# Cross-attention by pairs of heads on two row halves, with its projections interleaved in a new order

## What is computed

```python
def xattn(x, context):                       # x (4, 256, 128) normalised, context (4, 512, 256)
    q = split_heads(x @ Wq)                  # 16 heads of 64
    k, v = split(context @ Wkv)              # each (4, 16, 512, 64)
    k, v = concat(null_k, k), concat(null_v, v)        # one more key and value for every head
    attn = softmax(q * 64 ** -0.5 @ k.T)
    out = merge_heads(attn @ v) @ Wout
    return layernorm(out) * ln_scale + ln_bias
x = x + xattn(layernorm(x), ctx)
x = x + ffn(layernorm(x))                    # self-attention, router, 8 experts, top 2
```

## Time and profile before

| | us |
|---|---|
| median of 3 runs (715.19 to 719.41) | 719.25 |
| the profiled execution, its span | 711.4 |
| PE recorded busy | 602.2 (85%) |
| DVE | 587.9 (83%) |
| ACT | 454.6 (64%) |
| POOL | 227.9 (32%) |

### The profile page before, as it was taken

One profiled execution on the slowest core, in us unless ns is written; L12 is line 12 of the kernel. 1 busy time (PEld: TensorE's weight loads), 2 busy tenths in 40 slices (PEclk: granted clock), 3 DMA queues, 4 the chain that ended last, 5 costly groups with the idle time before them and its releaser, 6 DMA issues. The chain is left out here.

```text
span 711.4 us, 13311 instructions
## 1 busy us (share of the span) xinstructions
PE 602.2 (85%) x3580; PEld 492.3 (69%) x3580; DVE 587.9 (83%) x1282; ACT 454.6 (64%) x1094; POOL 227.9 (32%) x435
## 2 busy tenths in 40 slices
PE   2979889988999999899999336899997689797996
PEld 2757778767887778778787325666666577575885
DVE  4768899878898788998889747899983599979995
ACT  3657777766777677767777125888883356344563
POOL 1553334323333333333335354722132321414000
PEclk9989999999999999999999868999998699998999
DMA  8020000000000000000000002000000220200000
GB/s 255 17 54 2 2 29 3 1 1 0 0 30 0 1 0 0 0 0 1 1 1 1 1 4 82 1 1 0 0 0 1 78 77 2 77 1 0 0 0 29
DMA packets 15342, 13.48 MB, mean 19 GB/s; under 512 B 1984, under 2 KB 14656, under 8 KB 15296
## 3 DMA queue, kind: packets, MB, share of 16 engines
q1 hardware_dynamic: 15072, 12.94, 6.2%
q10 hardware_dynamic: 224, 0.03, 0.0%
HBM read 12.44 MB, written 0.52 MB: 18 GB/s over the span
## 5 line engine op out<-in xcount | busy, mean ns | idle before, releaser
L516 ACT ACTIVATE p_raw<-bank,bias 128x512 f32<-128x512 f32 x128 | 87.7, 688 | 43.1 <-DVE bias L587 39.4
L582 DVE TENSOR_REDUCE neg_max<-bank 128x1 f32<-128x512 f32 x128 | 86.9, 679 | 5.9 <-issue 4.0
L657 POOL TENSOR_SCALAR p_norm<-p_raw,rinv 128x512 f32<-128x512 f32 x128 | 87.0, 692 | 0.1
L606 DVE TENSOR_TENSOR pT_lo<-bank,pT_hi 128x512 fp32r<-128x512 f32 x128 | 82.4, 685 | 3.9 <-issue 2.3
L534 ACT ACTIVATE pT_hi<-bank 128x512 fp32r<-128x512 f32 x128 | 69.7, 599 | 24.9 <-PE bank L439 23.4
L1472 ACT ACTIVATE act_hi<-act_f 128x512 fp32r<-128x512 f32 x56 | 35.4, 632 | 58.9 <-DVE act_f L1515 58.8
L439 PE MATMUL bank<-ident,p_norm 128*128 128x128 f32 x512 | 66.8, 273 | 0.4 <-DVE pT_lo L606 0.4
L439 PEld LDWEIGHTS bank<-ident,p_norm 128*128 128x128 f32 x512 | 59.8, 141 | 9.3 <-issue 1.2
L451 PE MATMUL bank<-pT_hi,vals 128*128 128x256 f32 x256 | 64.9, 286 | 1.5 <-DVE o_lo L598 1.5
L451 PE MATMUL bank<-pT_lo,vals 128*128 128x256 f32 x256 | 64.0, 283 | 0.0
L426 PE MATMUL bank<-keys,q_hi 128*128 128x512 f32 x128 | 54.7, 427 | 3.0 <-ACT p_raw L516 2.8
(11 more groups left out here) (272 smaller groups left out, 1731.3 us busy)
## 6 DMA issues: line engine op xcount, KB each, us to landing
ctx_raw<-in_ctx SPq DMA_DIRECT2D x4, 512.0 KB, 4.7
wkv_raw<-in_L_xattn_Wkv SPq DMA_DIRECT2D x2, 1024.0 KB, 11.1
gu_raw<-in_L_ffn_w_gate SPq DMA_DIRECT2D x4, 448.0 KB, 3.6
gu_raw<-in_L_ffn_w_up SPq DMA_DIRECT2D x4, 448.0 KB, 4.3
dn_raw<-in_L_ffn_w_down SPq DMA_DIRECT2D x4, 448.0 KB, 5.1
wout_raw<-in_L_xattn_Wout SPq DMA_DIRECT2D x2, 512.0 KB, 14.8
x<-in_x SPq DMA_DIRECT2D x1, 512.0 KB, 6.8
wq_raw<-in_L_xattn_Wq SPq DMA_DIRECT2D x1, 512.0 KB, 10.2
```

Of the source, the lines that this page charges most:

```text
L516: act.activation(p_raw[:, h % 2, t, :], s_bank[t][:, :], ACT.Exp, bias=bias[:, h % H, t:t + 1], scale=X_SCALE, accum_out=row_sum[:, h % H, ...
L582: dve.tensor_reduce(neg_max[:, h % H, t:t + 1], s_bank[t][:, :], AX_X, ALU.max, negate=True).then_inc(max_s, 1)
L606: dve.tensor_tensor(pT_lo[:, h % 2, 2 * half:2 * half + 2, :], t_bank[half][:, :].rearrange("p (j n) -> p j n", j=2), f(pT_hi[:, h % 2, 2 ...
L657: pool.tensor_scalar(p_norm[:, h % 2, t, :], p_raw[:, h % 2, t, :], rinv[:, h % H, t:t + 1], 1.0, ALU.mult, ALU.mult).then_inc(p_norm_s, 1)
```

## The change

The cross-attention works on pairs of heads g (32 of them) in steps, with two heads of a pair on partitions 0 to 63 and 64 to 127.

- Query weights are stored once; one projection gives both heads' queries. Keys are kept as `keys_hi` and `keys_lo`, 8 tiles of two heads each. Scores are three matmuls of 64 rows for each head and token tile, alternating between the two heads, into two of four score banks.
- The two halves of the weighted values are copied by ACT (`o_copy`), added by DVE (`o_halves`) and split by GpSimd (`o_split`). The output projection runs for four pairs at once, in every fourth step, with `y_copy` by ACT for the first half of a batch and `y_add` by DVE for the second. The output weights are stored once.
- Every step with a successor projects one key unit and one value unit, four pairs ahead; queries, keys, values and context share `unit_bank`. For values ACT makes the high part and DVE the low part.
- The bias and the null terms are computed for two heads in one instruction. Probabilities are normalised in place.
- The loops over batches are written out on all engines. In the load stage the first key units are four instead of three, the splits of Wq and Wout have half the size, Wout is loaded once, and the null value's product has 8 matmuls of 128 rows instead of 16 of 64.

```diff
-            k.wq_hi, k.wq_lo = (sw(f"wq_{s}", [P, H, 2, DH]) for s in ("hi", "lo"))
+            k.wq_hi, k.wq_lo = (sw(f"wq_{s}", [P, H, DH]) for s in ("hi", "lo"))
-            k.wout_hi, k.wout_lo = (sw(f"wout_{s}", [P, H, D]) for s in ("hi", "lo"))
+            k.wout_hi, k.wout_lo = (sw(f"wout_{s}", [P, HP, D]) for s in ("hi", "lo"))
-            k.keys = sw("keys", [P, H, M])
+            k.keys_hi, k.keys_lo = (sw(f"keys_{s}", [P, HP, M]) for s in ("hi", "lo"))
...
-        s_bank, t_bank, y_bank, proj_bank = banks[0:2], banks[2:4], banks[6], banks[7]
-        q_whole, q_bank, o_bank = banks[4], banks[4][:, 0:N], banks[5][:, 0:N]
+        s_bank, t_bank, unit_bank, out_bank = banks[0:4], banks[4:6], banks[6], banks[7]
+        o_part, y_part = out_bank[:, 0:N], out_bank[:, N:2 * N]
+        AHEAD = HP // 2
+        QUART = 4
+        STEPS = range(-2, NP + 3)
...
+            def project_q(g):
...
+                b = g // HP
+                if unit_at(g - 2) is not None:
+                    pe.wait_ge(v_lo_s, g - 1)
+                elif g >= 1:
+                    pe.wait_ge(q_lo_s, g)
+                for i, (w, x) in enumerate(((k.wq_hi, k.xnT_hi), (k.wq_hi, k.xnT_lo), (k.wq_lo, k.xnT_hi))):
+                    last = pe.matmul(unit_bank[:, 0:N], w[:, columns(g), :].rearrange("p h d -> p (h d)"), x[:, b * N:(b + 1) * N],
+                                     start=i == 0, stop=i == 2)
+                last.then_inc(q_ps, 1)
...
+            def keys_unit(g):
...
+                pe.wait_ge(q_lo_s, g + 2)
+                if n // HP >= 1:
+                    pe.wait_ge(c_lo_s, n // HP * CT)
+                project(pe, k, "k", n % HP, 0, unit_bank).then_inc(k_ps, 1)
...
+            def values_unit(g):
...
+                pe.wait_ge(k_lo_s, g + 1)
+                project(pe, k, "v", n % HP // KT, n % KT, unit_bank).then_inc(v_ps, 1)
...
+            def scores(g, t):
...
+                G = 2 * g + t
+                if t == 0:
+                    pe.wait_ge(q_lo_s, g + 1)
+                    if g >= AHEAD:
+                        pe.wait_ge(k_lo_s, g - AHEAD + 1)
+                if G >= 2:
+                    pe.wait_ge(p_exp, 2 * G - 2)
+                for m, (q, keys) in enumerate(((q_hi, k.keys_hi), (q_lo, k.keys_hi), (q_hi, k.keys_lo))):
+                    for i in range(2):
+                        last = pe.matmul(score_bank(G, i)[:, :], q[rows(i), g % 2, t * P:(t + 1) * P], keys[rows(i), g % HP, :],
+                                         start=m == 0, stop=m == 2)
+                        if m == 2:
+                            last.then_inc(s_ps, 1)
...
+            def weighted_values(g, i):
...
+                pe.wait_ge(t_lo_s, 4 * g + 2 * i + 2)
...
+                if 2 * g + i >= 1:
+                    pe.wait_ge(o_raw_s, 2 * g + i)
...
+                for kt in range(KT):
+                    for n, x in enumerate((pT_hi, pT_lo)):
+                        last = pe.matmul(o_part, k.vals[:, kt, 2 * (g % HP) + i, :], x[:, i, kt, :],
+                                         start=kt == 0 and n == 0, stop=kt == KT - 1 and n == 1)
+                last.then_inc(o_ps, 1)
...
+            def project_out(s):
+
...
+                for j in range(QUART):
+                    g = QUART * m + j
...
+                    for n, (w, x) in enumerate(((k.wout_hi, o_hi), (k.wout_hi, o_lo), (k.wout_lo, o_hi))):
+                        last = pe.matmul(y_part, w[:, g % HP, :], x[:, g % O_KEPT, :], start=j == 0 and n == 0,
+                                         stop=m % 2 == 0 and j == QUART - 1 and n == 2)
...
+                last.then_inc(y_ps, 1)
...
+            for s in STEPS:
+                transpose_probs(s - 1, 1, 1)
+                if not after_context(s):
+                    keys_unit(s)
+                scores(s + 1, 1)
+                transpose_probs(s, 0, 0)
+                transpose_probs(s, 0, 1)
+                project_out(s)
+                if after_context(s):
+                    keys_unit(s)
+                    weighted_values(s - 1, 1)
+                    values_unit(s)
+                else:
+                    values_unit(s)
+                    weighted_values(s - 1, 1)
+                transpose_probs(s, 1, 0)
+                project_q(s + 2)
+                null_probs(s)
+                context_unit(s, 0)
+                weighted_values(s, 0)
+                scores(s + 2, 0)
+                context_unit(s, 1)
...
+            def values_head(g):
...
+                i, t = n % HP // KT, n % KT
+                act.wait_ge(v_ps, g + 1)
+                if n >= HP:
+                    act.wait_ge(o_ps, 2 * (n // KT * KT - KT))
+                act.activation(values_of(k, i, t, 0), by_head(unit_bank[:, :]), ACT.Copy).then_inc(v_hi_s, 1)
...
+            def o_copy(g, i):
...
+                act.wait_ge(o_ps, 2 * g + i + 1)
+                if g >= 2:
+                    act.wait_ge(o_sum_s, 2 * (g - 2) + i + 1)
+                act.activation(o_raw[:, g % 2, i, :], o_part, ACT.Copy).then_inc(o_raw_s, 1)
...
+            for s in STEPS:
+                probs_head(s - 1, 1, 1)
+                if not after_context(s):
+                    keys_head(s)
+                exponential(s + 1, 0, 0)
+                probs_head(s, 0, 0)
+                probs_head(s, 0, 1)
+                exponential(s + 1, 0, 1)
+                y_copy(s)
+                if after_context(s):
+                    keys_head(s)
+                    o_copy(s - 1, 1)
+                    values_head(s)
+                else:
+                    values_head(s)
+                    o_copy(s - 1, 1)
+                null_exponential(s + 1, 0)
+                q_head(s + 2)
+                null_head(s)
+                context_head(s, 0)
+                null_exponential(s + 1, 1)
+                probs_head(s, 1, 0)
+                exponential(s + 1, 1, 0)
+                exponential(s + 1, 1, 1)
+                o_copy(s, 0)
+                context_head(s, 1)
...
+            def values_tail(g):
...
+                i, t = n % HP // KT, n % KT
+                dve.wait_ge(v_hi_s, g + 1)
+                dve.tensor_tensor(values_of(k, i, t, 1), by_head(unit_bank[:, :]), f(values_of(k, i, t, 0)), ALU.subtract).then_inc(v_lo_s, 1)
...
+            def shift(g, t):
...
+                G = 2 * g + t
+                dve.wait_ge(max_s, 2 * G + 2)
+                dve.scalar_tensor_tensor(bias[:, t, columns(g)], neg_max[:, t, columns(g)], X_SCALE,
+                                         k.s0n[:, token_tile(G), columns(g)], ALU.mult, ALU.min).then_inc(bias_s, 1)
...
+            def o_halves(g, i):
...
+                dve.wait_ge(o_raw_s, 2 * g + i + 1)
+                if g >= 2:
+                    dve.wait_ge(o_lo_s, g - 1)
+                dve.tensor_tensor(o_sum[rows(i), g % 2, :], o_raw[0:DH, g % 2, i, :], o_raw[DH:P, g % 2, i, :], ALU.add).then_inc(o_sum_s, 1)
...
+            for s in STEPS:
+                probs_tail(s - 1, 1, 1)
+                if not after_context(s):
+                    keys_tail(s)
+                maximum(s + 1, 1, 0)
+                maximum(s + 1, 1, 1)
+                probs_tail(s, 0, 0)
+                shift(s + 1, 1)
+                probs_tail(s, 0, 1)
+                y_add(s)
+                if after_context(s):
+                    keys_tail(s)
+                o_halves(s - 1, 0)
+                o_halves(s - 1, 1)
+                values_tail(s)
+                q_tail(s + 2)
+                null_tail(s)
+                context_tail(s, 0)
+                inverse_sum(s + 1, 0)
+                probs_tail(s, 1, 0)
+                maximum(s + 2, 0, 0)
+                maximum(s + 2, 0, 1)
+                inverse_sum(s + 1, 1)
+                shift(s + 2, 0)
+                context_tail(s, 1)
...
+            def o_split(g):
...
+                pool.wait_ge(o_sum_s, 2 * g + 2)
+                if g >= O_KEPT:
+                    pool.wait_ge(y_ps, (g - O_KEPT) // QUART + 1)
+                pool.tensor_scalar(o_hi[:, g % O_KEPT, :], o_sum[:, g % 2, :], 1.0, 1.0, ALU.mult, ALU.mult).then_inc(o_hi_s, 1)
+                pool.wait_ge(o_hi_s, g + 1)
+                pool.tensor_tensor(o_lo[:, g % O_KEPT, :], o_sum[:, g % 2, :], f(o_hi[:, g % O_KEPT, :]), ALU.subtract).then_inc(o_lo_s, 1)
...
+            for s in STEPS:
+                whole_sum(s, 1)
+                normalise(s, 1, 0)
+                normalise(s, 1, 1)
+                normalise(s, 0, 1)
+                null_gap(s + 1, 0)
+                null_weight(s, 0)
+                o_split(s - 2)
+                null_weight(s, 1)
+                whole_sum(s + 1, 0)
+                null_gap(s + 1, 1)
+                normalise(s + 1, 0, 0)
```

More of the change, by code:

```diff
@@ L69, in token_stats, with project @@
     last.then_inc(done, 1)
[L74 to L82, removed]
-    if kind == "c":
[L84 to L89, removed]
+HP = H // 2
+NP = B * HP
+def project(pe, k, kind, i, t, out):
```

(47 more changed lines are left out.)

575 lines of the change are left out of this document (273 added, 302 removed).

## The result

| | before | changed |
|---|---|---|
| median of 4 runs each, us | 718.63 (715.19 to 719.41) | 729.89 (729.23 to 730.63) |
| ratio (95% interval) | | 1.0164 (1.0129 to 1.0199) |
| the profiled execution, its span | 711.4 | 727.4 |
| cross-attention complete (`yT`) | 398.1 | 408.5 |

The change makes the kernel 11.3 us, 1.6%, slower; the forecast was 3.5 us faster. In the profiled executions the cross-attention ends 10.4 us later than before. I first read it as the page and the windows show it.

The account below looks back on a forecast made before the run. Bound alternately by PE and the chain through ACT and DVE back to PE. 47.2 - 1.1 + 28 x 10.42 + 24.4 = 362.3, then attention's end 394.6 against 398.1: 719.25 - 3.5 = 715.8 us, range 699 to 731.

Parts of the forecast that it names:

- The plain step: One pair of heads in the cross-attention without extras: 8.93 us of PE work plus waits 1.45 and 0.04, 10.42 us.
- The new wait: PE's query projection waits for values_tail on DVE, queued behind the second o_halves addition: 1.45 us a step.
- The first transposes: Start of the first transposes in the cross-attention, after the fill: 47.2 us, give or take 0.8.
- A step with an output projection: Every fourth cross-attention step: 12 output projection matmuls add 1.42 us on PE.
- The score pairs: Two 64-row score matmuls on disjoint row halves overlap fully: 0.23 us a pair of 512 columns.
- T(0): Start of step 0's first transposes, forecast at 47.2 us.
- steps 9, 17 and 25: Null probabilities pass PE, ACT, DVE ahead of weighted_values: 1.45 us each, and 0.35 for three matmuls; 5.4 in all.
- the end of the attention: Cross-attention output yT complete at 394.6 us, against 398.1 before.
- steps 28 to 30: Cross-attention steps that project no units, bound by a loop from transposes through scores, maxima and normalisation: 7.0 us each.
- the tail behind T(31): From the last step's first transposes: transposes 0.9 us, then weighted values, copy, addition, split and last output matmuls 10.4.
- Rival 2: At o_halves on DVE: a POOL pass in front costs up to 0.68 us in 28 steps, 724 to 735; chance 0.10.
- Rival 4: Steps with extra work and the fill overlap more, or half of 24.4 and 1.0 of the end vanish: 704; chance 0.20.

Follow-up runs that it names:

- filled run: Changed kernel with five 512-column matmuls, unused by the result, added in front of each query projection in steps with units; 723.99 us, ratio 1.0084.
- the swap: Changed kernel with one line moved: on VectorE values_tail(s) goes ahead of o_halves(s-1,1); 699.11 us, ratio 0.9724.

## Why the prediction was wrong

**Right, by its own steps.** The plain step: 10.42 forecast, 10.42 measured. The new wait and its chain: 1.45 forecast, 1.49 measured (the mean of the weight loads' waits), with the addition directly ahead of the values' low part. The first transposes: 47.2 against 46.98. A step with an output projection: 10.42 + 1.42 against 11.84. The score pairs: 0.23 apart. DVE at 73%, below 80. The full overlap of pairs was taken from four 32-row matmuls, and it held for 64-row pairs too. The Trainium skill (TensorE: Matmul & The Clock Gate, "Measured speedup vs the span model") gives 3.07x for four 32-row tiles; the pairs here, 0.23 apart, do not agree with a stretch by it. Part of this is luck: T(0) stood anywhere from 46.9 to 49.7 in seven profiles, and between T(0) and T(28) errors cancelled (in the filled run, without falls, steps 9, 17 and 25 took 0.8 us less in all than their forecast, steps 10, 18 and 26, for which the sum had only the output projection, 2.2 more).

**Wrong: the end of the attention, 394.6 forecast, 408.5 measured, 13.9 us.** Put together from T(s):

| where | us |
|---|---|
| first transposes | -0.2 |
| six half-clock stretches, T(0) to T(28) | +8.7 |
| the rest of T(0) to T(28): 316.2 without falls, 315.1 forecast | +1.1 |
| step 30: an output projection that I forgot (steps 6, 10, ... 34 have one, the text counted six before step 28, and the last) | +1.4 |
| steps 28 to 30: 7.34, 7.34 and 7.3 without that projection, for 7.0 | +1.0 |
| the tail behind T(31): 13.2 for 11.3, at half clock from 405.0 | +1.9 |

The step that failed is a term that isn't there. The prediction put the price of a lower clock inside the attention at nothing: it counted every wait of PE as time alone, for a clock that the trace of before granted at 1.00 throughout. The runs showed six stretches at half clock in its place, 8.7 us. In before, PE had only six places with more than 1.4 us from one matmul's start to the next, one at a time and none above 1.88 (three of them are the row of L87 below, 1.6 in the record), and no fall. The change has a wait of 1.49 in almost every step, and in some a second one, or a longer one:
```profile
82.13 0.39 PE L434 MATMUL bank<-xnT_hi,wq_hi 128*128 128x256 f32 x1 [1.22 <-DVE vals L702]
82.47 0.29 PE L434 MATMUL bank<-xnT_hi,wq_lo 128*128 128x256 f32 x1
83.78 0.80 PE L82 MATMUL bank<-ident,ctx_raw 128*128 128x128 f32 x4 [1.02 <-DVE q_lo L687]
...
84.81 0.41 PE L511 MATMUL bank<-pT_hi,vals 128*128 128x256 f32 x1
85.02 0.41 PE L511 MATMUL bank<-pT_lo,vals 128*128 128x256 f32 x1
```
(timeline of PE in step 3 of the changed kernel), and in before, from its waits between 100 and 400 us (total, times, longest):
```profile
PE bank L87 <- DVE q_lo L577: 4.8, 3, 1.6
```
From one matmul's start to the next it had 1.49 us at steps 3 and 11 and then, 0.34 us of work later, 1.31; at 17 and 25 1.49 and 1.40; at 8 and 24 2.04 in one piece. At each of these six PE ran 3.41 us at half clock, beginning between 0.1 us ahead of the last wait's end and 1.3 us behind it: in the rows above matmuls of 256 columns start 0.21 us apart where 0.12 is usual. The filled waits show it to be so: the same waits for useful work, no falls, 8.7 us less. I had worked out each of those waits (1.2 and 1.45 for a step, 0.5 for values_head) and laid none beside the 1.45 that already stood in the same step. The Trainium skill (TensorE: Matmul & The Clock Gate, "A second HAM failure mode: psum-queue depth-cycling") tells of a kernel that cycled through PSUM banks, where small idle times of PE between groups of matmuls came often enough to make the clock swing. This trace agrees in the swing (six stretches at 0.50); here most of the waits are at one bank, `unit_bank`. It was not among my rivals.

The falls are 8.7 of the 13.9 us, and the sign does not hang on them alone. Without them the attention would have ended at 399.8, an estimate that the filled run bears out (402.2, less the 1.9 of its later start and 0.6 of its tail). That is 1.7 us behind before's, and not 3.5 ahead: the other 5.2 us are terms that the sum forgot (the projection at step 30) or had too small, the tail above all. Rival 2, a queue behind GpSimd, did not happen: the additions take 0.42 us as read. Rival 4, an overlap of the exceptional steps, went the other way, 1.1 us more. Between the medians the error is 14.8 us: 13.9 of the attention, and about 1 that no profile assigns.

**The larger lesson is in the same sum.** The prediction wrote that without the addition in front the stall would be 0.3 instead of 1.45. So it had the stall's 1.15 us a step in hand; the run gave 0.99. That one order holds 23.9 us of waits and 8.7 of clock; with the swap the ratio is 0.9724. The prediction used the number to explain the wait and did not ask what else could stand in its place.

## To carry to other kernels

When one PSUM bank serves in turn for several products, the low part that frees it belongs ahead of everything on its engine that waits for a later matmul. Waits of TensorE can cost more than their time when two come close together or one grows long (here 1.49 and 1.31, or 2.04 us): lay them side by side on one time line, keep a half-clock case with its own price among the rivals (here 1.46 us a place), and move independent work into them. Compare a profiled span with the spread of the runs before taking its difference for the change's.

## What the hardware showed that I had not expected

The same wait does not always bring the clock down. In the changed kernel PE had 2.036 us between two matmuls' starts at step 8 and 2.037 at step 16, with the same 1.67 us of work in the 3.43 around; at 142.13 the clock fell, at 236.93 it did not (the windows above). Steps 3, 11 and 19 had the same two gaps, and 19 had no fall; so it was with steps 9, 17 and 25 (1.49 and 1.40), of which 9 had none. Of nine such places six fell. The kernel with the additions on one half kept nearly the same gaps, and its profiled execution had one fall for the six, at step 16, where the changed kernel had none. Each fall between T(0) and T(28) lasted 3.41 us, in every profile. What decides it beyond the gaps stays open; a variant of such a kernel can gain or lose 1.5 us a place without its instructions being any slower. With the additions on one half the median fell by 6.0 us for an edit worth 3.6 by its steps.

The start varies too: the changed kernel and its six variants, whose code up to there is nearly the same, had their first transposes at 46.9 to 49.7 us over seven profiles, with 3.4 to 10.2 us at half clock from 36 us on. The time does not follow the half-clock stretches alone: the latest start (49.7) had 6.8 us of them, one at 48.8 had 10.2.
